# Routed expert tiles of 160 rows instead of 128, with the weights stationary in gate and up

## The chip, the cores and the metric

The kernel runs on one core of a Trainium2 chip. The metric is the device time of one execution in microseconds (us). The engines are TensorE (PE for its matmuls, PEld for its weight loads), VectorE (DVE), ScalarE (ACT), GpSimd (POOL) and SyncE (SP, which here only issues DMAs).

## What is computed

One block of a network on 512 tokens of width 1024: cross-attention, a gated feed-forward with ternary weights, and a mixture of experts. The last part is the one that matters here:

```python
h = _rmsnorm(x, rms_weight)
ht = h.reshape(-1, d)                      # 512 x 1024
topv, topi = jax.lax.top_k(softmax(ht @ router_w), 2)
# w_dense: the two normalised weights of each token, else 0
g = jnp.einsum('td,edf->tef', ht, w_gate)  # 8 experts, 1024 -> 512
u = jnp.einsum('td,edf->tef', ht, w_up)
eo = jnp.einsum('tef,efd->ted', jax.nn.silu(g) * u, w_down)  # 512 -> 1024
moe = jnp.einsum('te,ted->td', w_dense, eo)
sh = jax.nn.silu(ht @ sw_gate) * (ht @ sw_up) @ sw_down      # shared expert
return x + (moe + sh)
```

Each token goes through two of the eight experts, so there are 1024 routed rows. Evaluating the reference's inputs gives 123, 138, 144, 135, 89, 129, 152 and 114 rows for the eight experts.

## The kernel before

**Arithmetic.** Every fp32 operand is split into a high part and a low part (the difference), both stored as fp32r. A product is three matmuls: high x high, high x low, low x high. ScalarE makes the high part of a weight (line L1465, `WH`, by `split`), VectorE the low part (line L980, `WL`).

**Tiles.** The expert stage works in tiles of 128 rows. Tiles 0 to 2 are the shared expert on the first 384 tokens. The routed tiles follow, grouped by expert: an expert with n rows has ceil(n/128) tiles, here 13 in all. The last tile, `total`, is the shared expert on tokens 384 to 511. The numbers of tiles are found on the chip (`CNT`) and steer loops on every engine: an outer loop over the eight experts, an inner loop over the tiles of one. Rows are scattered by token into a DRAM buffer `rows_dram` (GpSimd, line L647) at places that are padded to whole tiles, and the padding is zeroed before by 34 DMAs of 256 KB (line L573). At the end GpSimd gathers two result rows for each token (line L657, `GA` and `GB`) and VectorE adds them, weighted (lines L1172, L1175).

**One routed tile on TensorE** (function `tile` of the tensor block). The rows stand transposed in `ETH` and `ETL` (high, low; 128 x 8 x 128) as the stationary operand, and the weights stream past 512 columns at a time. Gate goes to bank 0 and up to bank 1, each with 16 matmuls of `ETH` (lines L299, L300, by `highs`) and 8 of `ETL` (L305, by `lows`). Then come 4 transposes of the next tile's rows `XG` (L1843), 4 of the hidden values `HE` (L1885), 4 more of `XG`, and the down product: 16 matmuls with `HTH`, 8 with `HTL`, into banks 2 and 3.

**The others in one routed tile.** ScalarE: copies half of the last result to `YS` (L1517), SiLU of gate (L1521), `HTH` (L1526), `ETH` (L1500). VectorE: the other half of `YS` (L1023), gate times up (L994), `HTL` (L1002), `ETL` (L987). After the last tile of an expert both split the next expert's weights, six pieces of 128 x 2048: two for gate, two for up, two for down. ScalarE waits with the two for down until the down product that reads the old ones is done. SyncE stores `YS` and loads `XG` for the tile after next, and loads the weights of the expert after next, one piece as each raw buffer becomes free.

**Order at the seam** between the shared tiles and the first routed one: VectorE subtracts the first half of expert 1's gate weights, does the last shared tile's hidden values, then the second half of the gate weights, then `ETL` of the first routed tile. TensorE waits for each half of the gate weights by itself (`free_c[0]`, `free_c[1]`), and for `ETL` only ahead of the 8 low matmuls.

## Time and profile before

| | |
|---|---|
| median of three runs | 668.27 us (668.19 to 670.72) |
| profiled execution, own time | 670.5 us |
| its span, first to last instruction | 668.7 us |
| mean granted TensorE clock | 0.99 of full |

The routed tiles take 394 to 633 us of the span. Busy shares are means over stages; for one change the waits and the starts of single instructions in its own stage say more. A matmul's recorded duration includes its way through the array, so the distance between the starts of two neighbours is what one costs in a stream.

### The profile page before, as it was taken

Reading aid. Unit: us, or ns where it says so; the run is one execution under the profiler, and the core shown is the slowest. Engines: PE = TensorE matmul, PEld = TensorE weight load, DVE = VectorE, ACT = ScalarE, POOL = GpSimd, SP = SyncE. Lnnn points to the kernel's source line nnn. Section 1 sums busy time; section 2 is a strip of 40 time slices with the busy share of each in tenths; the row PEclk is TensorE's granted clock in tenths of the full one; section 3 lists DMA queues with packets and bytes.
Section 4 is the critical chain, followed back from the end, with each engine's and each line's share of the span. In section 5 each row is a group of like instructions: output and inputs, shape, how many; then the busy total and the mean of one; then the engine's idle time right before and its main releaser. Section 6 shows DMA issues by size and latency. Waiting matters only on the chain.

```text
span 668.7 us, 9683 instructions
## 1 busy us (share of the span) xinstructions
PE 635.5 (95%) x3288; PEld 477.4 (71%) x3289; DVE 488.0 (73%) x789; ACT 413.8 (62%) x538; POOL 144.7 (22%) x140
## 2 busy tenths in 40 slices
PE   6889999998999999969999999999999999999996
PEld 5778888886886444434477877878878788787774
DVE  5788888879687779988898386547291992745886
ACT  3898888789647879875573366254361781816640
POOL 3354445406000334529200400000000000000051
PEclk9899999999999999979999999999999999999999
DMA  8967776765176988529975749929283796482946
GB/s 336 363 276 296 296 289 238 310 269 168 53 261 268 419 346 361 195 86 397 397 301 204 287 181 385 372 79 392 93 333 137 276 390 274 168 334 97 373 162 248
DMA packets 31113, 179.02 MB, mean 268 GB/s; under 512 B 3824, under 2 KB 3824, under 8 KB 14832
## 3 DMA queue, kind: packets, MB, share of 16 engines
q1 hardware_dynamic: 26064, 161.39, 62.4%
q0 software_dynamic: 5024, 17.30, 6.8%
q8 instruction: 14, 0.23, 0.1%
q14 instruction: 11, 0.09, 0.0%
HBM read 155.62 MB, written 23.07 MB: 267 GB/s over the span
## 4 chain that ended last, share of the span: by engine, by line
PE 54%; DVE 17%; ACT 15%; DMA 6%; issue 6%; POOL 1%; SPq 1%; DVEq 1%; POOLq 0%; ACTq 0%
PE BK L299 11%; PE BK L300 11%; PE BK L305 11%; PE BK L293 9%; ACT PR L1280 5%; ACT RA L1253 3%; PE BK L1762 3%; PE BK L1661 2%; DVE WL L980 2%; DMA RA<-wbit 2%; PE BK L1885 2%; DMA GA<-rows,SLOT 2%; DMA RX<-wqk 1%; DVE BH L862 1%; PE BK L1646 1%
## 5 line engine op out<-in xcount | busy, mean ns | idle before, releaser
L299 PE MATMUL BK<-WH,ETH 128*128 128x512 f32 x272 | 107.4, 395 | 1.3 <-ACT ETH L1500 1.3
L300 PE MATMUL BK<-WL,ETH 128*128 128x512 f32 x272 | 106.1, 390 | 0.0
L980 DVE TENSOR_TENSOR WL<-RA,WH 128x2048 fp32r<-128x2048 f32 x40 | 89.4, 2287 | 9.7 <-ACT WH L1465 9.5
L1465 ACT ACTIVATE WH<-RA 128x2048 fp32r<-128x2048 f32 x40 | 73.8, 1923 | 2.3 <-PE BK L1762 2.3
L305 PE MATMUL BK<-WH,ETL 128*128 128x512 f32 x272 | 67.5, 390 | 0.0
L1526 ACT ACTIVATE HTH<-BK 128x256 fp32r<-128x256 f32 x30 | 10.7, 383 | 88.7 <-PE BK L1885 88.6
L299 PEld LDWEIGHTS BK<-WH,ETH 128*128 128x128 f32 x272 | 51.0, 188 | 15.8 <-DVE WL L980 3.3
L657 POOL DMA_INDIRECT GA<-rows,SLOT x4 | 4.9, 1228 | 264.7 <-DVE WL L980 263.8
L305 PEld LDWEIGHTS BK<-WH,ETL 128*128 128x128 f32 x272 | 51.0, 188 | 10.7
L300 PEld LDWEIGHTS BK<-WL,ETH 128*128 128x128 f32 x272 | 51.1, 188 | 10.3
L994 DVE TENSOR_TENSOR HE<-BK,SI 128x256 f32<-128x256 f32 x34 | 12.9, 420 | 57.0 <-PE BK L305 48.3
L625 POOL TENSOR_TENSOR HB<-HB,ND (+2 forms) x28 | 31.1, 1127 | 104.9 <-DVE BH L862 104.2
L1350 ACT ACTIVATE RA<-RA,RT 128x2048 int16<-128x2048 f32 x22 | 44.2, 2018 | 9.6 <-DMA RA<-wbit 6.6
L299 PE MATMUL BK<-WH,HTH 128*128 128x512 f32 x120 | 48.1, 401 | 0.0
L300 PE MATMUL BK<-WL,HTH 128*128 128x512 f32 x120 | 46.9, 391 | 0.0
L980 DVE TENSOR_TENSOR WL<-RC,WH 128x2048 fp32r<-128x2048 f32 x20 | 44.9, 2285 | 0.6 <-ACT WH L1465 0.6
L1716 PE MATMUL BK<-TG,XQ 128*128 128x512 bf16 x192 | 42.4, 379 | 0.1
L1762 PE MATMUL BK<-TD,HQT 128*128 128x512 bf16 x176 | 39.4, 384 | 0.0
L1465 ACT ACTIVATE WH<-RC 128x2048 fp32r<-128x2048 f32 x20 | 37.3, 1920 | 0.6 <-PE BK L305 0.6
L1280 ACT ACTIVATE PR<-BK,RT 128x512 f32<-128x512 f32 (+1 forms) x64 | 32.7, 536 | 6.6 <-DVE RT L729 6.6
L1253 ACT ACTIVATE RA<-RA 128x2048 f32<-128x2048 f32 x19 | 36.2, 1912 | 0.0
L1716 PE MATMUL BK<-TX,XQ 128*128 128x512 bf16 x160 | 35.2, 379 | 0.0
(272 smaller groups left out, 1400.9 us busy)
## 6 DMA issues: line engine op xcount, KB each, us to landing
RA<-wbit SPq DMA_DIRECT2D x54, 1024.0 KB, 6.3
RA<-wmoe SPq DMA_DIRECT2D x40, 1024.0 KB, 6.8
RC<-wmoe SPq DMA_DIRECT2D x20, 1024.0 KB, 7.6
rows<-ZERO POOLq DMA_DIRECT2D x34, 256.0 KB, 12.1
XG<-rows SPq DMA_DIRECT2D x15, 512.0 KB, 7.1
rows<-YS SPq DMA_DIRECT2D x14, 512.0 KB, 6.6
RA<-wqk SPq DMA_DIRECT2D x7, 640.0 KB, 8.1
RA<-wo SPq DMA_DIRECT2D x4, 1024.0 KB, 7.5
```

Source lines behind the costliest of these rows:

```text
L293: m = e.matmul(dst, st, mv, start=first and i == 0 and j == 0, stop=last and i == n - 1 and j == 2)
L299: e.matmul(dst, sh, mh, start=first and i == 0, stop=False)
L300: e.matmul(dst, sh, ml, start=False, stop=False)
L305: m = e.matmul(dst, sl, mh, start=False, stop=i == len(pairs) - 1)
L625: e.tensor_tensor(HB[:, t, cs], HB[:, t, cs], ND[:, cs], ALU.mult).then_inc(s("hnd"), 1)
L980: e.tensor_tensor(WL[m][:, q * RAW:q * RAW + RAW], RC[j][:, :], WH[m][:, q * RAW:q * RAW + RAW].bitcast(f32), ALU.subtract)\
L1253: e.activation(RA[j][:, :], RA[j][:, :], ACT.Abs, accum_out=ACCW[:, column]).then_inc(free_a[j], 1)
L1280: ins = e.activation(PR[h][:, off:off + P * (i + 1)], STR[h][:, off:off + P * (i + 1)], ACT.Exp, bias=NM[:, h, i:i + 1], accum_out=RS[:, h ...
L1350: e.activation(RB16[j], RB[j][:, :], ACT.Copy, scale=SW[:, 0:1]).then_inc(s("rnd"), 1)
L1465: e.activation(WH[m][:, q * RAW:q * RAW + RAW], RC[2 * m + q][:, :], ACT.Copy)\
L1716: m = e.matmul(bank[out], XQ[:, k, t * P:t * P + P], weights[:, k, :], start=k == 0, stop=k == KD - 1)
L1762: m = e.matmul(bank[2 * (t % 2) + q], HQT[t % 2][:, k, :], (TD1[:, k, :] if k < 16 else TD2[:, k - 16, :])[:, q * 512:q * 512 + 512], star ...
```

## The change

A routed tile now has R = 160 rows. An expert has 1 tile for up to 160 rows, so the eight experts have 8 tiles.

- **Gate and up** have the weights stationary (128 x 128 blocks) and stream the rows: `EX` holds for each of the 8 blocks of the width 160 high values and then 160 low ones. Each block of `WH` streams all 320 columns, each block of `WL` the 160 high ones. There are 4 blocks of hidden columns (f) by 8 blocks of width (k), for gate and for up. The result stands transposed already (hidden column by row), so the transposes of `HE` fall away.
- The two halves of each result (high rows and low rows) are added on the way: ScalarE copies one half of gate to `SR`, VectorE adds the other (`gate_sum`), ScalarE takes the SiLU, and VectorE does the product with both halves of up (`routed_product`).
- **Up goes into the banks of gate**, so it waits for `gate_sum` (semaphore `hsum`).
- **Down** has the first 128 rows as before. The last 32 rows' high parts and low parts stand side by side in `HX` and go through as one stationary block of 64 columns against `WH`, plus one of 32 columns against `WL`; both halves are added by `result` on their way out, in `XY`.
- The rows' transposes are 16 in place of 8 (128 rows and 32 rows apart), their loads and the result's stores are two DMAs in place of one.
- A routed tile waits for all of `EX` and for both halves of the gate weights before it starts. At the seam VectorE does `routed_lo(NS)` ahead of the second half of the gate weights, and TensorE does all 16 row transposes ahead of the `HE` transposes. `XG` and `XY` now lie where `H3` lay.
- Zeroing takes 40 DMAs in place of 34.
- The last shared tile waits for both parts of its rows before its first matmul.

```diff
-MAXT = NS + (2 * TOK // P + NE - 1)
+R = 160
+TAIL_R = R - P
+MAXT = NS + NE + (2 * TOK - 1) // R
...
+NZERO = (XT_TILES - NS) * R // (P // 2)
+TK = ((0, 1, 2), (3, 4, 5), (6, 7))
+TB = (0, 1, 3)
+TB_FIRST = (4, 5, 3)
+GBK = (0, 1, 3, 4)
+AB = (2, 5)
...
-        XG = c("XG", [P, DM], f32)
-        assert c.at == TG[0].manual_sbuf_range[0]
+        EX = c("EX", [P, KD, 2, R], f32r)
+        UT = c("UT", [P, 3, R], f32)
+        HX = nc.alloc_sbuf_tensor_at("HX", [P, KE, 2 * R], f32r, offset=HTH.manual_sbuf_range[0])
...
+        SR = Region(a.at)("SR", [P, KE, R], f32)
...
+        XG = kept("XG", [P, DM], f32)
+        XY = kept("XY", [P, DM], f32)
+        XTAIL, YTAIL = slice(0, TAIL_R), slice(TAIL_R, 2 * TAIL_R)
...
+            e.dma_start(rows_dram[bass.ds(row, P), :], H3[:, NS, :]).then_inc(s("x_in3"), 16)
             e.wait_ge(s("rows"), 1)
...
+            e.wait_ge(s("et_pe"), 2 * NS)
+            e.dma_start(XG[:, :], rows_dram[R:R + P, :]).then_inc(s("e_in"), 16)
+            e.wait_ge(s("x_in3"), 32)
+            e.dma_start(XY[XTAIL, :], rows_dram[R + P:2 * R, :]).then_inc(s("e_in"), 16)
...
+            def store(t):
+                row, tail = e.snap((t - NS) * R), e.snap((t - NS) * R + P)
+                waits(e, ("ys_a", t + 1), ("ys_d", t + 1), ("y_st", t * 32 + 32))
+                e.dma_start(rows_dram[bass.ds(row, P), :], YS[:, :]).then_inc(s("y_st"), 16)
+                e.dma_start(rows_dram[bass.ds(tail, TAIL_R), :], XY[YTAIL, :]).then_inc(s("y_st"), 16)
...
-            for half in range(2 * (XT_TILES - NS)):
+            for half in range(NZERO):
...
+            def routed_lo(t, at=TB):
+                for n, ks in enumerate(TK):
+                    e.wait_ge(s("et_hi"), t * 3 + n + 1)
+                    ins = e.tensor_tensor(EX[:, ks[0]:ks[-1] + 1, 1, :], r3(bank[at[n]][:, 0:R * len(ks)], len(ks)),
+                                          EX[:, ks[0]:ks[-1] + 1, 0, :].bitcast(f32), ALU.subtract)
+                    if n != 1:
+                        ins.then_inc(s("et_lo"), 1)
+
+            def gate_sum(t, q):
+                waits(e, ("gate_a", t * 3 + q + 1))
+                v = SR[:, 2 * q:2 * q + 2, :]
+                e.tensor_tensor(v, routed_columns(2 * q, 2, 0), v, ALU.add).then_inc(s("hsum"), 1)
+
+            def routed_product(t):
+                waits(e, ("gate_a", t * 3 + 3))
+                for n, (f, m) in enumerate(((0, 2), (2, 1), (3, 1))):
+                    waits(e, ("up_pe", t * 4 + f + m))
+                    v, u = SR[:, f:f + m, :], UT[:, f % 3:f % 3 + m, :]
+                    e.tensor_tensor(u, routed_columns(f, m, 0), v, ALU.mult)
+                    e.tensor_tensor(v, routed_columns(f, m, 1), v, ALU.mult).then_inc(s("hsum"), 1)
+                    waits(e, ("hsum", t * 5 + n + 3))
+                    ins = e.tensor_tensor(v, u, v, ALU.add)
+                    if n != 1:
+                        ins.then_inc(s("eh"), 1)
+
+            def routed_hidden_lo(t):
+                for q in range(2):
+                    ks = slice(2 * q, 2 * q + 2)
+                    e.wait_ge(s("ht_hi"), t * 2 + q + 1)
+                    ins = e.tensor_tensor(HX[:, ks, R + TAIL_R:2 * R], SR[:, ks, 0:P], HX[:, ks, 0:P].bitcast(f32),
+                                          ALU.subtract)
+                    if q == 0:
+                        ins.then_inc(s("ht_lo"), 1)
+                e.tensor_tensor(HX[:, :, R:R + TAIL_R], SR[:, :, P:R], HX[:, :, P:R].bitcast(f32), ALU.subtract)\
+                    .then_inc(s("ht_lo"), 1)
 
             def hidden_product(t):
-                waits(e, ("esilu", t + 1), ("up_pe", t + 1))
+                waits(e, ("gate_a", t * 3 + 3), ("up_pe", t * 4 + 4))
                 for q in range(2):
                     cs = slice(q * 256, q * 256 + 256)
                     e.tensor_tensor(HE[:, cs], bank[1][:, cs], SI[:, cs], ALU.mult).then_inc(s("eh"), 1)
...
-                e.tensor_copy(YS[:, 512:1024], bank[3]).then_inc(s("ys_d"), 1)
+                waits(e, ("y2_pe", t + 1), ("y_st", t * 32 + 32))
+                e.tensor_copy(YS[:, 512:1024], bank[AB[1]])
+                waits(e, ("ys_a", t + 1))
+                for q in range(2):
+                    v = XY[YTAIL, q * 512:q * 512 + 512]
+                    ins = e.tensor_tensor(v, bank[6 + q][YTAIL, :], v, ALU.add)
+                ins.then_inc(s("ys_d"), 1)
 
             def router_evac(t):
...
             e.wait_ge(s("rows"), 1)
             hidden(NS - 1, HTKH, HTKL)
+            routed_lo(NS, TB_FIRST)
             split(1, 0, (1,))
-            rows_lo(NS)
             split(1, 1)
+            e.sem_inc(s("hsum"), 5 * NS)
 
             def tile(t):
+                gate_sum(t, 0)
                 result(t)
-                hidden(t)
-                rows_lo(t + 1)
+                gate_sum(t, 1)
+                routed_product(t)
+                routed_hidden_lo(t)
...
+            def routed_hi(t, at=TB):
+                for n, ks in enumerate(TK):
+                    if n < 2:
+                        e.wait_ge(s("et_pe"), t * 2 + n + 1)
+                    e.activation(EX[:, ks[0]:ks[-1] + 1, 0, :], r3(bank[at[n]][:, 0:R * len(ks)], len(ks)), ACT.Copy)\
+                        .then_inc(s("et_hi"), 1)
             e.wait_ge(s("d_pe"), 2 * NT)
             split(0, None, (1,), (0,))
...
@@ -1513,30 +1589,48 @@
             split(0, None, (2,), (1,))
 
             def result(t):
-                waits(e, ("y2_pe", t + 1), ("y_st", t * 16 + 16))
-                e.activation(YS[:, 0:512], bank[2], ACT.Copy).then_inc(s("ys_a"), 1)
-
...
-                e.wait_ge(s("gate_pe"), t + 1)
-                e.activation(SI[:, :], bank[0], ACT.Silu).then_inc(s("esilu"), 1)
-                if hi is HTKH:
+                waits(e, ("y2_pe", t + 1), ("y_st", t * 32 + 32), ("et_lo", t * 2 + 2))
+                e.activation(YS[:, 0:512], bank[AB[0]], ACT.Copy)
+                for q in range(2):
+                    ins = e.activation(XY[YTAIL, q * 512:q * 512 + 512], bank[6 + q][XTAIL, :], ACT.Copy)
+                ins.then_inc(s("ys_a"), 1)
+
+            def hidden(t, n, hi=HTH):
+                e.wait_ge(s("gate_pe"), t * 2 + 2)
+                e.activation(SI[:, :], bank[0], ACT.Silu).then_inc(s("gate_a"), 3)
+                if n == NS - 1:
                     split(1, NS, (0,))
...
-                if more:
+                if n < NS - 1:
                     rows_hi(t + 1)
+
             def tile(t):
                 result(t)
-                hidden(t)
-            hidden(0)
+                for q in range(2):
+                    waits(e, ("gate_pe", t * 2 + q + 1))
+                    e.activation(SR[:, 2 * q:2 * q + 2, :], routed_columns(2 * q, 2, 1), ACT.Copy)\
+                        .then_inc(s("gate_a"), 1)
+                for q in range(2):
+                    ks = slice(2 * q, 2 * q + 2)
+                    waits(e, ("hsum", t * 5 + q + 1))
+                    ins = e.activation(SR[:, ks, :], SR[:, ks, :], ACT.Silu)
+                ins.then_inc(s("gate_a"), 1)
+                for q in range(2):
+                    ks = slice(2 * q, 2 * q + 2)
...
-                                    IDF[:, :])
+                    m = e.transpose(bank[4 + q][:, k * P:k * P + P], rows[:, cs], IDF[:, :])
                 m.then_inc(s("et_pe"), 1)
+
+            def routed_rows(t, ns, at=TB):
+                for n in ns:
+                    if n == 0:
+                        waits(e, ("e_in", t * 32 + 32))
+                    for i, k in enumerate(TK[n]):
+                        cs = slice(k * P, k * P + P)
+                        e.transpose(bank[at[n]][:, i * R:i * R + P], XG[:, cs], IDF[:, :])
+                        m = e.transpose(bank[at[n]][:, i * R + P:i * R + R], XY[XTAIL, cs], IDF[XTAIL, XTAIL])
+                    if n != 1:
...
+            def routed_tile(t, gi):
+
+                waits(e, ("et_lo", t * 2 + 2))
+                for m in range(2):
+                    waits(e, (free_c[2 * m], gi + 1), (free_c[2 * m + 1], gi + 1))
+                    for f in range(KE):
+                        if m and f % 2 == 0:
+                            waits(e, ("hsum", t * 5 + f // 2 + 1))
+                        for k in range(KD):
+                            at = slice(k * FE + f * P, k * FE + f * P + P)
+                            if k == KD - 1:
+                                e.matmul(bank[GBK[f]][:, 0:R], WL[m][:, at], EX[:, k, 0, :], start=False, stop=False)
+                            mm = e.matmul(bank[GBK[f]][:, 0:2 * R], WH[m][:, at],
+                                          EX[:, k, :, :].rearrange("p a b -> p (a b)"), start=k == 0, stop=k == KD - 1)
+                            if k < KD - 1:
+                                e.matmul(bank[GBK[f]][:, 0:R], WL[m][:, at], EX[:, k, 0, :], start=False, stop=False)
+                        if m:
+                            mm.then_inc(s("up_pe"), 1)
+                        elif f % 2:
+                            mm.then_inc(s("gate_pe"), 1)
+                waits(e, ("hsum", t * 5 + 3))
+                routed_rows(t + 1, (0, 1))
+                waits(e, ("hsum", t * 5 + 4))
+                routed_rows(t + 1, (2,))
                 waits(e, ("ys_a", t + 1), ("ys_d", t + 1), (free_c[4], gi + 1), (free_c[5], gi + 1))
                 for h in range(2):
                     waits(e, ("ht_hi", t * 2 + h + 1))
                     for q in range(2):
-                        highs(e, bank[2 + q], y_high(h, q), h == 0)
+                        highs(e, bank[AB[q]], [(HX[:, k, 0:P], WH[2][:, down_at(k, q)], WL[2][:, down_at(k, q)])
+                                               for k in (2 * h, 2 * h + 1)], h == 0)
                 e.wait_ge(s("ht_lo"), t * 2 + 2)
                 for q in range(2):
-                    m = lows(e, bank[2 + q], y_low(q))
-                m.then_inc(s("y2_pe"), 1)
+                    lows(e, bank[AB[q]], [(HX[:, k, R + TAIL_R:2 * R], WH[2][:, down_at(k, q)]) for k in range(KE)])
+                for q in range(2):
+                    for k in range(KE):
+                        if k:
+                            e.matmul(bank[6 + q][XTAIL, :], HX[:, k, P:R], WL[2][:, down_at(k, q)], start=False, stop=False)
+                        mm = e.matmul(bank[6 + q][0:2 * TAIL_R, :], HX[:, k, P:R + TAIL_R], WH[2][:, down_at(k, q)],
+                                      start=k == 0, stop=k == KE - 1)
+                        if k == 0:
+                            e.matmul(bank[6 + q][XTAIL, :], HX[:, k, P:R], WL[2][:, down_at(k, q)], start=False, stop=False)
+                mm.then_inc(s("y2_pe"), 1)
...
-            tile(total, NE + 1, None, False)
+            tile(total, NS, NE + 1)
 
 
```

**TensorE, one routed tile: gate.** Before, the start of a tile in the loop (BK is a PSUM bank, WH_145 and WL_146 the gate weights):

```order
L299 MATMUL BK<-WH_145,ETH 128x512
L300 MATMUL BK<-WL_146,ETH 128x512
L299 MATMUL BK<-WH_145,ETH 128x512
L300 MATMUL BK<-WL_146,ETH 128x512
L305 MATMUL BK<-WH_145,ETL 128x512 x8
```

After, the start of a tile, the first of the four blocks f and the change to the second:

```order
L2015 MATMUL BK<-EX,WH_145 128x320
L2018 MATMUL BK<-EX,WL_146 128x160
L2015 MATMUL BK<-EX,WH_145 128x320
L2018 MATMUL BK<-EX,WL_146 128x160
L2014 MATMUL BK<-EX,WL_146 128x160
L2015 MATMUL BK<-EX,WH_145 128x320 x2
```

The 512 columns of weights that streamed past the rows have become 320 and 160 columns of rows that stream past blocks of weights; each matmul loads another block.

**TensorE, the end of a routed tile's down product after** (before, it ended with the row of x8):

```order
L317 MATMUL BK<-WH_141,HX 128x512 x8
L2040 MATMUL BK<-WH_141,HX 64x512
L2043 MATMUL BK<-WL_151,HX 32x512
L2039 MATMUL BK<-WL_151,HX 32x512
L2040 MATMUL BK<-WH_141,HX 64x512
```

The matmuls with 64 and 32 output rows are new, 8 of each in a tile.

**VectorE at the seam** (HE: hidden values of the last shared tile; WL_146: gate weights of the first expert, WL_150 its up weights). Before:

```order
L980 TENSOR_TENSOR WL_146<-RA_95,WH_145 128x2048
L994 TENSOR_TENSOR HE<-BK,SI 128x256 x2
L1002 TENSOR_TENSOR HTKL<-BK,HTKH 128x256 x2
L980 TENSOR_TENSOR WL_146<-RA_96,WH_145 128x2048
L987 TENSOR_TENSOR ETL<-BK,ETH 128x512 x2
L980 TENSOR_TENSOR WL_150<-RA_97,WH_140 128x2048
```

After:

```order
L1004 TENSOR_TENSOR WL_146<-RA_95,WH_145 128x2048
L1054 TENSOR_TENSOR HE<-BK,SI 128x256 x2
L1062 TENSOR_TENSOR HTKL<-BK,HTKH 128x256 x2
L1017 TENSOR_TENSOR EX<-BK,EX 128x3x160 x2
L1017 TENSOR_TENSOR EX<-BK,EX 128x2x160
L1004 TENSOR_TENSOR WL_146<-RA_96,WH_145 128x2048
L1004 TENSOR_TENSOR WL_150<-RA_97,WH_140 128x2048
```

The second half of the gate weights has moved behind the low part of the first routed tile's rows.

## Rows read from the trace of the kernel before

**Rows 1.** The page's part 1: busy time, share of the span, instructions.

```profile
PE 635.5 (95%) x3288; PEld 477.4 (71%) x3289; DVE 488.0 (73%) x789; ACT 413.8 (62%) x538; POOL 144.7 (22%) x140
```

**Rows 2.** Busy time by stretch: engines, clock, DMA share, GB/s; inside the routed tiles.

```profile
420.00:440.00 20.00, 19.85 (x94) 16.29 (x93) 7.37 (x10) 2.90 (x6) 0.00 (x0) 1.00 0.73 297
```

**Rows 3.** Groups by line and shape, 405.2 to 625.7 us (twelve routed tiles).

```profile
L1843 PE MATMUL BK<-IDF,XG 128*128 128x128 f32 x96 | 14.4, 272 | 0.0
...
L980 DVE TENSOR_TENSOR WL<-RA,WH 128x2048 fp32r<-128x2048 f32 x28 | 62.3, 2287 | 7.0 <-ACT WH L1465 7.0
L1465 ACT ACTIVATE WH<-RA 128x2048 fp32r<-128x2048 f32 x28 | 51.4, 1927 | 0.0
...
L987 DVE TENSOR_TENSOR ETL<-BK,ETH 128x512 fp32r<-128x512 f32 x24 | 15.5, 686 | 0.8
...
L1500 ACT ACTIVATE ETH<-BK 128x512 fp32r<-128x512 f32 x24 | 13.0, 600 | 0.0
...
L994 DVE TENSOR_TENSOR HE<-BK,SI 128x256 f32<-128x256 f32 x24 | 9.1, 420 | 47.8 <-PE BK L305 47.0
```

**Rows 4.** Timeline (start, us): first and last routed tile's end of up; what follows.

```profile
405.21 0.60 PE L1843 MATMUL BK<-IDF,XG 128*128 128x128 f32 x4
...
625.78 0.60 PE L1843 MATMUL BK<-IDF,XG 128*128 128x128 f32 x4
...
628.57 5.54 ACT L1465 ACTIVATE WH<-RA 128x2048 fp32r<-128x2048 f32 x3
630.53 4.49 DVE L980 TENSOR_TENSOR WL<-RA,WH 128x2048 fp32r<-128x2048 f32 x2 [1.00 <-ACT WH L1465]
...
631.25 1.98 PE L305 MATMUL BK<-WH,HTL 128*128 128x512 f32 x8
...
633.07 0.40 PE L299 MATMUL BK<-WH,ETH 128*128 128x512 f32 x1
```

**Rows 5.** Timeline of PE in narrow windows: attention matmuls of falling width (L1661).

```profile
64.89 0.46 PE L1661 MATMUL BK<-PTH,VH 128*128 128x384 f32 x2
...
65.06 0.46 PE L1661 MATMUL BK<-PTH,VH 128*128 128x256 f32 x3
...
65.18 0.46 PE L1661 MATMUL BK<-PTH,VH 128*128 128x256 f32 x3
...
65.47 0.44 PE L1661 MATMUL BK<-PTH,VL 128*128 128x512 f32 x1
...
65.75 0.57 PE L1661 MATMUL BK<-PTH,VL 128*128 128x512 f32 x2
```

**Rows 6.** Timeline at the seam: last shared tile into first routed tile.

```profile
390.95 0.60 PE L1843 MATMUL BK<-IDF,XG 128*128 128x128 f32 x4
...
391.24 0.76 DVE L994 TENSOR_TENSOR HE<-BK,SI 128x256 f32<-128x256 f32 x2 [0.76 <-PE BK L305]
...
393.29 2.29 DVE L980 TENSOR_TENSOR WL<-RA,WH 128x2048 fp32r<-128x2048 f32 x1
...
394.20 0.49 PE L299 MATMUL BK<-WH,ETH 128*128 128x512 f32 x1 [1.27 <-ACT ETH L1500]
```

**Rows 7.** PE's longest idle time (timeline), and busy time with clock just then.

```profile
289.54 2.72 PE L1756 MATMUL BK<-IDB,HQ 128*128 128x128 bf16 x19 [5.41 <-DVE HQ L966]
...
290.00:294.00 4.00, 3.83 (x25) 2.32 (x23) 2.85 (x5) 3.29 (x4) 0.00 (x0) 0.52 0.55 233
```

**Rows 8.** Timeline of the end: last subtractions ahead of the gathers, first gather, last wait.

```profile
635.94 4.49 DVE L980 TENSOR_TENSOR WL<-RA,WH 128x2048 fp32r<-128x2048 f32 x2
...
641.39 2.10 POOL L657 DMA_INDIRECT GA<-rows,SLOT  x1 [263.81 <-DVE WL L980]
...
661.83 1.28 DVE L1172 SCALAR_TENSOR_TENSOR XRES<-GA,RT,XRES 128x1024 f32<-128x1024 f32 x1 [1.18 <-DMA GA<-rows,SLOT]
```

**Rows 9.** Zeroing: its DMAs (page, part 6), and busy time just behind them.

```profile
rows<-ZERO POOLq DMA_DIRECT2D x34, 256.0 KB, 12.1
...
334.00:337.00 3.00, 3.00 (x22) 2.10 (x20) 3.00 (x3) 1.18 (x1) 0.00 (x0) 1.00 0.15 31
```

More of the change, by code:

```diff
@@ L1557, in _ @@
             split(NE + 1, total, (2,))
-            hidden(total, False)
+            hidden(total, NS)
         @blk.tensor
@@ L1856, in routing, with tile @@
                     logits_t()
-            def tile(t, gi, rows=None, more=True):
-                waits(e, ("et_hi", t * 2 + 2), (free_c[0], gi + 1))
+            def tile(t, n, gi):
+                more = n < NS
+                waits(e, ("et_hi", t * 3 + 3), (free_c[0], gi + 1))
+                if not more:
+                    waits(e, ("et_lo", t * 2 + 2))
                 for m in range(2):
@@ L1863, in tile @@
                             waits(e, (free_c[2 * m + q], gi + 1))
[L1864 removed]
+                        highs(e, bank[m], [(EX[:, k, 0, 0:P], WH[m][:, k * FE:k * FE + FE], WL[m][:, k * FE:k * FE + FE])
                                            for k in range(4 * q, 4 * q + 4)], q == 0)
[L1866 removed]
+                        if n == 0:
                             routing((m, q))
                     e.wait_ge(s("et_lo"), t * 2 + 2)
[L1869 to L1871 removed]
+                    lows(e, bank[m], [(EX[:, k, 1, 0:P], WH[m][:, k * FE:k * FE + FE]) for k in range(KD)])\
+                        .then_inc(s(("gate_pe", "up_pe")[m]), (2, 4)[m])
+                    if n == 0:
                         routing((m, 2))
[L1873 to L1874 removed]
+                if n < NS - 1:
+                    rows_t(0, H3[:, n + 1, :])
+                elif more:
+                    e.wait_ge(s("ys_d"), NS)
+                    routed_rows(NS, (0, 1, 2), TB_FIRST)
                 else:
@@ L1877, in tile @@
                     kept_result(HT1H, HT1L, 2)
-                if isinstance(t, int) and t == 0:
+                if n == 0:
                     ranks()
@@ L1945, in _ @@
             for t in range(NS):
[L1946 removed]
+                tile(t, t, 0)
             e.wait_ge(s("cnt"), 1)
```

118 lines of the change are left out of this document (55 added, 63 removed).

## The prediction

> **What bounds the kernel now.** I read the page first: TensorE is busy 95% of the span [rows 1]. Then busy time by stretch inside the routed tiles: 19.85 of 20 us, clock 1.00, DMA share 0.73 [rows 2]. So in the stage that changes TensorE is the bound, and the others matter only where they make it wait. The groups by line there show how VectorE waits for TensorE: 47.8 us ahead of gate times up [rows 3]. The timeline gives the price: the end of up comes at 405.21 us in the first routed tile and at 625.78 in the thirteenth, so one tile takes 220.57 / 12 = 18.38 us; the first routed gate matmul starts at 394.20 [rows 6] and the last down product ends at 633.07 [rows 4]. Thirteen tiles take 238.9 us.
>
> **The change, first the number of tiles.** Of the expected row counts (123, 138, 144, 135, 89, 129, 152, 114) five lie above 128 and none above 160: 13 tiles become 8.
>
> **Prices of a matmul.** I take the distance of starts. Eight of 512 columns take 633.07 - 631.25 = 1.82, so 0.23 each [rows 4]. 384 columns cost 0.17 and 256 cost 0.12; from 65.18 to 65.75 lie one of 256, two of 128 and one of 512, which leaves 0.22 for the two narrow ones: 0.11 each [rows 5]. The row transposes, also 128 wide, cost (0.60 - 0.27) / 3 = 0.11 as well [rows 3, 4]. The slope between 256 and 512 columns is 0.43 ns a column, so 128 columns alone would need 0.06: below some 250 columns the loading of the next weight block sets the pace, at 0.11. For the new shapes: 320 columns lie between 256 and 384, 0.145; 160 columns get the floor, 0.11. Both matmuls of a pair load a new block, so a pair costs 0.255. Bounds: 0.215 if the narrow one cost only its columns (0.07), 0.29 if the two cost as 384 and 256 (0.17, 0.12).
>
> The Trainium skill, "TensorE: Matmul & The Clock Gate", section "Back-to-back issue gap", has about 81 ns for a load and a matmul of 128 columns in a stream, and 131 ns for 512. The trace says 110 and 230, so the measurement decides.
>
> **TensorE in a new tile.** Gate 32 pairs 8.15, up 8.15; row transposes 16 x 0.11 = 1.75; down as before 24 x 0.23 = 5.5; the new tail of down 16 x 0.23 = 3.7 (512 columns stream past 64 or 32 columns of weights, which costs as much as past 128). Sum 27.25. The HE transposes and the wait ahead of them are gone.
>
> **The others in a new tile.** Let T be the moment at which up is issued. VectorE costs 0.42 for 256 and 0.69 for 512 columns, so 0.49 for 320, 0.32 for 160, 0.65 for 480; ScalarE 0.60 for 512 and 1.93 for 2048, so 0.44 for 320 and 0.57 for 480 [rows 3]; weight pieces in a row take 2.2 on VectorE (4.49 for two) and 1.8 on ScalarE (5.54 for three) [rows 4].
> - T + 0.3 the last up matmul is out (0.40 recorded) [rows 4]. VectorE: two products and an add for the last 160, until T + 1.35. ScalarE: high part of the hidden values T + 1.8, then three pieces of EX, T + 3.45.
> - TensorE transposes until T + 1.75 and needs the hidden values then: no wait of note. Down lasts until T + 10.95.
> - VectorE: low parts until T + 4.4, then waits for ScalarE's first weight piece (3.45 + 1.9 = T + 5.4). Both gate pieces are through at T + 9.9, 1 us ahead of the next gate at T + 10.95. This is what hides them; without it each us late costs 1 us in each of 8 tiles.
> - ScalarE's pieces for down wait for T + 11.2 and take until T + 15.
> - VectorE's six pieces end at T + 18.7, and only then comes `gate_sum`, T + 19.2. TensorE ends gate at T + 19.1 and must wait for it, since up goes into the same banks: a wait of 0.1 to 0.2. The second `gate_sum`, behind three operations of 0.69, ends near T + 21.8; up's third block needs it at T + 23.4.
> So a tile takes 27.5, with VectorE just behind TensorE. Eight take 220.0: **-18.9**.
>
> Loads and stores: a weight piece is asked for at T + 7.7 at the earliest and T + 18.7 at the latest, and used 27.5 us after its predecessor; the extra DMAs for the tails stand in SP's queue behind waits that are over early. The DMA share was 0.73 with a faster cycle [rows 2]. Nothing.
>
> **The seam.** Before, the last shared tile's up ends at 390.95, VectorE subtracts the second half of the gate weights from 393.29 to 395.6, and gate has started at 394.20, since it needed that half later and ETL later still [rows 6]. After: 16 transposes until 392.7, seen at 393.0; ScalarE's remaining EX pieces (0.57, 0.44) until 394.0, its hidden halves until 394.7; VectorE's HTKL until 395.2, EX low 1.7, until 396.9, second half of the gate weights 2.3, until 399.2. Gate starts at 399.3: **+5.1** (bounds 4 and 6).
>
> That leaves TensorE idle for about 6 us (393.3 to 399.3). Its one comparable idle time was 5.41 us, and in the work behind it the granted clock was 0.52, the 1.2 GHz level, over the stretch 290 to 294 [rows 7]. Four us at half pace give back two: **+2.0** (bounds 0 and 4).
>
> **The end.** Before, the last two pieces ahead of the gathers run from 635.94 to 640.43, and the first gather starts at 641.39 [rows 8]; against the end of down (633.07) that is 7.4 and 8.3 later. After, VectorE's result waits for three ScalarE copies (0.3 + 3 x 0.6, less overlap: 1.8), then two adds (1.3), then two pieces (4.5): 7.8. The end waits for the gathers (661.83) [rows 8], so **+0.5**. The last shared tile's own wait for its rows' low parts (T + 4.4 against T + 10.95) is covered by the long down product.
>
> **Zeroing.** Six more DMAs of 256 KB are 1.6 MB behind 8.9; behind them the DMA share falls to 0.15 for 3 us [rows 9], which takes them up. Nothing (bound 1).
>
> **The sum.** +5.1 + 2.0 - 18.9 + 0.5 = -11.3. Against its own execution (span 668.7, time 670.5) this is a span of 657.4 and a time of 659.2. That execution was 2.2 above the median 668.27, so I forecast 657.0.
>
> **The rivals.**
> - **A: as summed**, 657. Its own range 652 to 664: the seam and the clock 3 either way, 0.3 a tile for the small operations.
> - **B: the narrow matmul hides its weight load under the wide one before it.** For it: two loads of 0.11 just fit into 0.215. Against it: in rows 5 a 128-wide matmul behind others costs 0.11. Gate then ends at T + 17.8, `gate_sum` still at T + 19.2, up takes 6.9: a cycle of 26.1, 11 less in all: 646. By the skill's 81 ns the pair would be about 0.22 and the result much the same.
> - **C: VectorE becomes the bound (slower).** Place: the first `gate_sum` behind six subtractions. Between T and T + 19.2 stand 13 further short operations on two engines that hand over to each other; a hand-over that costs 0.1 to 0.2 more than I allow comes straight on TensorE's wait, in 8 tiles. From 1.4 us a tile the gain is gone. At 2 us: 673. For it: no slack. Against it: the hand-over HE to TensorE is short now and VectorE's durations are steady.
> - **D: pairs at their upper price**, 0.29: 2.2 a tile, 17.9 in all: 675. Rows 5 speak against it.
> - **E: small sums**: a longer time at the low clock, DMAs that land late, a stall at each loop border: 665 to 669.
>
> **How the numbers follow.** A 0.62, B 0.12, C 0.12, D 0.06, E 0.08. The likeliest is A. The range 646 to 669 takes in A, B and E and leaves out C and D, near 2 in 10. Half a per cent, 3.3 us, is about what a measurement of this kernel can tell from no change; within it lie 665 to 671.6. That has E and the upper edge of A: 0.13. Slower: C and D, 0.17. Faster: 0.70.
>
> **What would show it.** Right: 8 ends of up 27.5 apart; starts of 320 and 160 wide matmuls 0.145 and 0.11 apart; first routed gate matmul near 399.3 behind an idle time of 6 us, at a clock near 0.5; TensorE's only repeated wait a small one for `gate_sum`. Wrong: pairs of 0.215 or 0.29; TensorE waits of over 1 us a tile for `gate_sum`, for the gate weights or for EX; a clock that falls again inside the tiles; waits for DMA.

## The result, and the profile after

The changed kernel takes 683.66 us (median of 4 runs, 683.05 to 685.42) against 668.96 (4 runs) of the kernel before: ratio 1.022, 95% interval 1.0191 to 1.025. It is slower: the interval lies above 1. The forecast was 657.0, range 646 to 669: the time lies outside the range, on the other side of no change.

The profiled execution has a span of 683.6, 14.9 longer than before. First the page's part 1; it answers to [rows 1].

```profile
PE 649.1 (95%) x3663; PEld 498.8 (73%) x3677; DVE 513.6 (75%) x861; ACT 424.6 (62%) x559; POOL 148.3 (22%) x146
```

TensorE is the bound as before. Of its longest waits in the changed kernel (us in total, times, longest) only the middle row belongs to the routed tiles, and that one stands at the seam. Inside the routed tiles it waits for nobody: from 420 to 640 us it is busy 20.00 of every 20 us.

```profile
PE BK L1664 <- ACT WVH L1274: 6.5, 1, 6.5
PE BK L2015 <- DVE WL L1004: 5.3, 1, 5.3
PE BK L1850 <- DVE HQ L990: 5.2, 1, 5.2
```

So the time is in TensorE's own work. The timeline of TensorE after (start, duration) shows one whole tile: gate starts, the row transposes start, down starts, its last 32 rows start, the next gate starts. The last row is the end of the eighth tile.

```profile
433.93 0.31 PE L2015 MATMUL BK<-EX,WH 128*128 128x320 f32 x1
434.08 0.24 PE L2018 MATMUL BK<-EX,WL 128*128 128x160 f32 x1
434.15 0.35 PE L2015 MATMUL BK<-EX,WH 128*128 128x320 f32 x1
434.34 0.24 PE L2018 MATMUL BK<-EX,WL 128*128 128x160 f32 x1
...
450.41 0.27 PE L1944 MATMUL BK<-IDF,XG 128*128 128x128 f32 x1
450.61 0.24 PE L1945 MATMUL BK<-IDF,XY 32*128 32x32 f32 x1
450.79 0.33 PE L1944 MATMUL BK<-IDF,XG 128*128 128x128 f32 x1
451.05 0.24 PE L1945 MATMUL BK<-IDF,XY 32*128 32x32 f32 x1
451.22 0.33 PE L1944 MATMUL BK<-IDF,XG 128*128 128x128 f32 x1
...
453.82 0.50 PE L311 MATMUL BK<-WH,HX 128*128 128x512 f32 x1
...
456.10 0.63 PE L311 MATMUL BK<-WH,HX 128*128 128x512 f32 x1
456.53 0.63 PE L312 MATMUL BK<-WL,HX 128*128 128x512 f32 x1
...
458.02 0.39 PE L312 MATMUL BK<-WL,HX 128*128 128x512 f32 x1
458.25 0.39 PE L311 MATMUL BK<-WH,HX 128*128 128x512 f32 x1
...
460.97 0.39 PE L2040 MATMUL BK<-WH,HX 128*64 128x512 f32 x1
...
464.65 0.31 PE L2015 MATMUL BK<-EX,WH 128*128 128x320 f32 x1
...
648.97 0.39 PE L311 MATMUL BK<-WH,EX 128*128 128x512 f32 x1
```

Reading the differences of starts, beside what was forecast:

| part of a tile | measured | forecast |
|---|---|---|
| gate and up, 128 matmuls | 450.41 - 433.93 = 16.48 | 16.3 |
| 16 row transposes | 453.82 - 450.41 = 3.41 | 1.75 |
| down, 24 matmuls | 460.97 - 453.82 = 7.15 | 5.5 |
| down, last 32 rows, 16 matmuls | 464.65 - 460.97 = 3.68 | 3.7 |
| tile | 30.72 | 27.5 |

Two parts are wrong, and by the same size. A 32-row transpose starts 0.26 behind the 128-row one ahead of it (450.79 to 451.05), and the next 128-row one 0.17 behind that (451.05 to 451.22): 0.43 for a pair that was forecast at 0.22. And matmuls of 512 columns in the down product lie 0.43 apart (456.10 to 456.53), where 0.23 was forecast and is measured a moment later (458.02 to 458.25). Busy time by stretch after shows the clock in both. The columns are the stretch, its length, PE, PEld, DVE, ACT, POOL, the granted clock, the DMA share and GB/s; the stretches are gate and up, the transposes, the first part of down, and the rest of down.

```profile
444.00:450.40 6.40, 6.40 (x52) 6.40 (x51) 2.26 (x6) 0.47 (x1) 0.00 (x0) 1.00 0.66 252
450.40:453.80 3.40, 3.40 (x17) 2.06 (x16) 2.41 (x7) 0.93 (x2) 0.00 (x0) 1.00 0.00 0
454.40:457.80 3.40, 3.40 (x10) 2.65 (x8) 2.20 (x3) 3.40 (x4) 0.00 (x0) 0.50 0.63 193
458.00:464.60 6.60, 6.60 (x30) 4.37 (x29) 6.60 (x4) 4.03 (x3) 0.00 (x0) 1.00 0.65 245
```

Behind the transposes the clock is at the 1.2 GHz level for 3.4 us, in every one of the eight tiles (it falls at 423.6, 454.4, 485.1, 515.8, 546.5, 577.3, 608.0 and 638.7), although PE counts as busy all through. Look also at PEld in the second row: 2.06 of 3.40, where gate and up have 6.40 of 6.40. During the mixed transposes the weight loads no longer lie end to end. In the busy times that is the only sign of the loss.

The pair of gate and up costs what was forecast, 16.48 / 64 = 0.2575 against 0.255, but not in the way that was forecast. From the start of a 320-wide matmul to the next start lie 0.19 (434.15 to 434.34) in place of 0.145, and from a 160-wide one 0.07 (434.08 to 434.15) in place of 0.11. Both loads of a pair lie end to end there (PEld 6.40 of 6.40). The sum came out right and the split did not; what sets the split was not looked at.

At the seam, which answers to [rows 6], the timeline after reads:

```profile
390.70 0.27 PE L1944 MATMUL BK<-IDF,XG 128*128 128x128 f32 x1
...
394.11 0.65 PE L1993 MATMUL BK<-IDF,HE 128*128 128x128 f32 x4
...
395.43 0.76 DVE L1062 TENSOR_TENSOR HTKL<-BK,HTKH 128x256 fp32r<-128x256 f32 x2 [3.67 <-ACT HTKH L1606]
...
396.10 1.61 DVE L1017 TENSOR_TENSOR EX<-BK,EX 128x480 fp32r<-128x480 f32 x3
...
397.62 4.49 DVE L1004 TENSOR_TENSOR WL<-RA,WH 128x2048 fp32r<-128x2048 f32 x2
...
400.05 0.60 PE L2015 MATMUL BK<-EX,WH 128*128 128x320 f32 x1 [5.29 <-DVE WL L1004]
```

Gate starts at 400.05, 5.85 later than before, behind an idle time of 5.29; the order of VectorE's steps is the forecast's, each 0.7 to 1.0 late, because the 16 transposes end at 394.11 in place of 392.7. The clock is low until 406.6, and the first tile's gate and up take 19.58, 3.1 more than the others'.

The budget of the span against the forecast of 657.4: transposes 8 x 1.66 = 13.3; low clock in down 8 x 1.65 = 13.2; gate and up 8 x 0.18 = 1.4; clock behind the seam 1.1; seam 0.75; no wait for `gate_sum` -2.0 (8 x 0.25); the end -1.5. Sum 26.2, and 657.4 + 26.2 = 683.6.

### The profile page after: what moved, and what is told of

Read it like the earlier page. It is cut to its first block, busy times and chain, and to the rows that moved or that the text cites. A ratio compares the mean times of both kernels' runs of the same rounds, so it can differ in the third digit from the quotient of the medians.

```text
span 683.6 us, 10567 instructions
## 1 busy us (share of the span) xinstructions
PE 649.1 (95%) x3663; PEld 498.8 (73%) x3677; DVE 513.6 (75%) x861; ACT 424.6 (62%) x559; POOL 148.3 (22%) x146
## 4 chain that ended last, share of the span: by engine, by line
PE 61%; DVE 15%; ACT 12%; DMA 4%; issue 4%; POOL 1%; SPq 1%; DVEq 0%; POOLq 0%; ACTq 0%
PE BK L2015 14%; PE BK L305 9%; PE BK L2018 5%; PE BK L311 5%; ACT PR L1349 5%; PE BK L312 4%; PE BK L317 3%; PE BK L1755 3%; PE BK L1856 3%; PE BK L1944 3%; PE BK L2040 2%; PE BK L1945 2%; DVE WL L1004 2%; PE BK L2039 2%; DMA RA<-wbit 2%
## 5 line engine op out<-in xcount | busy, mean ns | idle before, releaser
L2015 PE MATMUL BK<-EX,WH 128*128 128x320 f32 x512 | 134.7, 347 | 5.3 <-DVE WL L1004 5.3
L2018 PE MATMUL BK<-EX,WL 128*128 128x160 f32 x448 | 106.9, 239 | 0.0
L2015 PEld LDWEIGHTS BK<-EX,WH 128*128 128x128 f32 x512 | 93.9, 192 | 6.2 <-issue 5.5
L2018 PEld LDWEIGHTS BK<-EX,WL 128*128 128x128 f32 x448 | 87.2, 195 | 0.3
L1625 ACT ACTIVATE HX<-SR 128x320 fp32r<-128x320 f32 x16 | 7.5, 471 | 57.6 <-DVE SR L1035 57.6
L1032 DVE TENSOR_TENSOR UT<-BK,SR 128x160 f32<-128x160 f32 (+1 forms) x24 | 9.1, 380 | 39.1 <-PE BK L2015 39.1
L1810 PEld LDWEIGHTS BK<-TG,XQ 128*128 128x128 bf16 x192 | 18.6, 98 | 22.5 <-ACT XQ L1412 0.6
L311 PE MATMUL BK<-WH,HX 128*128 128x512 f32 x64 | 33.4, 523 | 0.0
L607 POOL TENSOR_TENSOR WQH<-RA,ONEF 128x768 fp32r<-128x768 f32 (+1 forms) x14 | 22.1, 1576 | 51.2 <-DMA RA<-wqk 43.4
L1856 PEld LDWEIGHTS BK<-TD,HQT 128*128 128x128 bf16 x176 | 17.4, 100 | 20.8 <-issue 1.7
```

Source lines behind the costliest of these rows:

```text
L311: e.matmul(dst, sh, mh, start=first and i == 0, stop=False)
L1810: m = e.matmul(bank[out], XQ[:, k, t * P:t * P + P], weights[:, k, :], start=k == 0, stop=k == KD - 1)
L1856: m = e.matmul(bank[2 * (t % 2) + q], HQT[t % 2][:, k, :], (TD1[:, k, :] if k < 16 else TD2[:, k - 16, :])[:, q * 512:q * 512 + 512], star ...
L2015: mm = e.matmul(bank[GBK[f]][:, 0:2 * R], WH[m][:, at], EX[:, k, :, :].rearrange("p a b -> p (a b)"), start=k == 0, stop=k == KD - 1)
L2018: e.matmul(bank[GBK[f]][:, 0:R], WL[m][:, at], EX[:, k, 0, :], start=False, stop=False)
```

## The experiments

**e1_full_rows: transposes of one shape.** The 32 tail rows are loaded into the last 32 partitions of `XY`, and the transpose reads all 128 partitions of it; the 96 columns that nobody wants are overwritten by the transpose of `XG` that follows. The number of matmuls, of weight loads and of bytes moved by DMA stays.

```diff
-                e.dma_start(XY[XTAIL, :], rows_dram[bass.ds(tail, TAIL_R), :]).then_inc(s("e_in"), 16)
+                e.dma_start(XY[XIN, :], rows_dram[bass.ds(tail, TAIL_R), :]).then_inc(s("e_in"), 16)
...
-                        e.transpose(bank[at[n]][:, i * R:i * R + P], XG[:, cs], IDF[:, :])
-                        m = e.transpose(bank[at[n]][:, i * R + P:i * R + R], XY[XTAIL, cs], IDF[XTAIL, XTAIL])
+                        e.transpose(bank[at[n]][:, i * R + TAIL_R:i * R + R], XY[:, cs], IDF[:, :])
+                        m = e.transpose(bank[at[n]][:, i * R:i * R + P], XG[:, cs], IDF[:, :])
```

> The changed kernel (683.7), but the transposes of the last 32 rows read all 128 partitions of their tile (the 32 rows moved to its upper end, the rest is overwritten), so that all 16 row transposes have one shape. Theory 1, the change between 128-row and 32-row weight loads is what makes 16 transposes take 3.41 us, and this slow stretch is what the clock falls after: transposes 1.75 us, no fall of the clock in the down products, a tile of 27.4 us, eight times 3.3 less: about 657. Theory 2, the clock falls because of the load-bound gate and up matmuls or of the half-empty tail of down: transposes 1.75 us, but the down product still has its 3.4 us at the low level, a tile of 29.1: about 670.

Measured: 656.98 us (654.8 to 657.76), ratio to before 0.9807 (0.9784 to 0.9831); span 655.3. The 16 transposes take 1.67, the clock stays at 1.00 inside the tiles, down takes 5.57, a tile 27.40 (428.31 to 455.70). Busy time by stretch of this kernel, transposes and the down product behind them:

```profile
444.80:446.40 1.60, 1.60 (x16) 1.60 (x16) 1.22 (x4) 0.46 (x2) 0.00 (x0) 1.00 0.00 0
446.50:450.00 3.50, 3.50 (x18) 2.87 (x17) 2.61 (x6) 3.50 (x5) 0.00 (x0) 1.00 0.53 184
```

PEld is busy 1.60 of 1.60. One edit takes away both losses, 3.3 us a tile and 26.7 us in all: without the mixed transposes the clock does not fall inside the tiles either.

**e2_grouped: the same transposes, sorted by shape.** In each of the three groups first those of 128 rows, then those of 32: 5 changes of shape inside the stretch in place of 15.

```diff
                         e.transpose(bank[at[n]][:, i * R:i * R + P], XG[:, cs], IDF[:, :])
+                    for i, k in enumerate(TK[n]):
+                        cs = slice(k * P, k * P + P)
                         m = e.transpose(bank[at[n]][:, i * R + P:i * R + R], XY[XTAIL, cs], IDF[XTAIL, XTAIL])
```

> The changed kernel, but in each group of blocks the 128-row transposes come first and then the 32-row ones: 6 changes of shape in place of 16. Theory 1a, each change between the shapes costs about 0.2 us: the 16 transposes take about 2.4 us. Theory 1b, a 32-row transpose is slow by itself whatever stands next to it: 3.4 us as before. The clock falls less or not at all if the length of the stretch decides: 662 to 676; at 1b 683.

Measured: 659.14 (one run), below the 662 that was expected at least; transposes 2.10 a tile (2.4 expected), no fall of the clock inside the tiles. TensorE's timeline of this kernel:

```profile
499.97 0.49 PE L1944 MATMUL BK<-IDF,XG 128*128 128x128 f32 x3
500.39 0.37 PE L1947 MATMUL BK<-IDF,XY 32*128 32x32 f32 x3
500.69 0.55 PE L1944 MATMUL BK<-IDF,XG 128*128 128x128 f32 x3
501.17 0.37 PE L1947 MATMUL BK<-IDF,XY 32*128 32x32 f32 x3
501.47 0.44 PE L1944 MATMUL BK<-IDF,XG 128*128 128x128 f32 x2
501.83 0.31 PE L1947 MATMUL BK<-IDF,XY 32*128 32x32 f32 x2
```

From the first of 128 rows to the first of 32 it takes 0.42; two steps of 0.11 in it leave 0.20 for the change. (In the second group 501.17 - 500.69 = 0.48 leave 0.26.) Three of 32 rows and the change back take 500.69 - 500.39 = 0.30; with 0.17 for the change back, as in the changed kernel, those among their own kind cost some 0.07. It is the change between the two kinds of transpose that costs, not the small transpose.

**e3_filler: the mixed stretch cut by dense matmuls.** Four matmuls of 512 columns, into banks that are overwritten later, stand behind the first and behind the second group of mixed transposes of each tile.

```diff
+            def filler():
+                for q in range(2):
+                    for u in range(2):
+                        e.matmul(bank[6 + q], WH[1][:, 0:P], WH[1][:, 0:512], start=True, stop=True)
...
-                routed_rows(t + 1, (0, 1))
+                routed_rows(t + 1, (0,))
+                filler()
+                routed_rows(t + 1, (1,))
+                filler()
```

> The changed kernel with 8 more dense matmuls of 512 columns in each routed tile (1.84 us of work whose result is overwritten), four behind the first and four behind the second group of row transposes. Theory 1, the unbroken slow stretch makes the clock fall: it falls no more or less, and a tile gets 0.2 us longer at most: 680 to 686, though work was added. Theory 2, gate and up or the tail are the cause: the clock falls as before and each tile is 1.84 longer: about 698.

Measured: 686.55 (one run; 680 to 686 expected), mean clock 0.990 against 0.967. The stretch with its fillers takes 1.24 + 1.03 + 1.24 + 1.03 + 0.81, down 5.57, a tile 31.08. Busy time by stretch of this kernel, over the transposes and over down:

```profile
450.40:456.00 5.60, 5.60 (x26) 3.94 (x26) 2.18 (x6) 2.22 (x5) 0.00 (x0) 1.00 0.07 11
456.20:460.00 3.80, 3.80 (x18) 3.14 (x17) 2.73 (x3) 3.80 (x3) 0.00 (x0) 1.00 0.40 148
```

The clock no longer falls inside the tiles, so 2.06 us of useless work a tile cost only 0.36 (the run is still 2.9 us slower than the changed kernel). The mixed transposes themselves still cost their 0.43 a pair.

**e4_before_short: the mixing put into the kernel before.** Six transposes of 32 rows are added between those of 128 in each routed tile; they write what the next one overwrites.

```diff
+                    if rows is None and k < 3:
+                        e.transpose(bank[4 + q][:, k * P + P:k * P + P + 32], XG[0:32, cs], IDF[0:32, 0:32])
```

> The kernel before (668.3) with six 32-row transposes added per routed tile between the 128-row ones of the rows (results overwritten): nothing of the change but this mix. Theory 1: each costs about 0.3 us beyond nothing, 1.9 to 2.6 a tile, and the clock falls behind them for up to 1.7 more: 13 tiles, 693 to 722, mean clock under 0.98. Theory 2: 693 to 702 and no fall of the clock inside the routed tiles.

Measured: 686.88 (one run), below both expected ranges. The twelve transposes of a tile (8 of rows, 4 of `HE`) and the wait among them take 3.17 with the six added ones, in place of 1.76: 0.235 net for each. TensorE's timeline, of the kernel before and then of this one:

```profile
441.92 0.60 PE L1843 MATMUL BK<-IDF,XG 128*128 128x128 f32 x4
442.67 0.77 PE L1885 MATMUL BK<-IDF,HE 128*128 128x128 f32 x4
```

```profile
445.43 0.27 PE L1843 MATMUL BK<-IDF,XG 128*128 128x128 f32 x1
445.63 0.24 PE L1846 MATMUL BK<-IDF,XG 32*128 32x32 f32 x1
...
446.84 0.60 PE L1887 MATMUL BK<-IDF,HE 128*128 128x128 f32 x4
```

Before, four row transposes (0.44) and a wait of 0.31 lie ahead of `HE`. With three small ones among them the four take 446.84 - 445.43 = 1.41, so each added one costs (1.41 - 0.44) / 3 = 0.32, as in the changed kernel (0.43 - 0.11), and covers part of that wait. So the price is there without anything else of the change. The clock did not fall in any tile: the mixing by itself is not enough for that.

**e5_double: as long a stretch, but of one shape.** In e1's kernel each of the 16 transposes is issued twice, to the same place.

```diff
+                        for u in range(2):
```

> The kernel with full row transposes (e1_full_rows), in which each of the 16 transposes of a routed tile is issued twice, to the same place: 32 transposes of one shape at 0.105 each, a stretch of about 3.4 us, as long as the mixed one in the changed kernel (3.41), but without gaps. The output is not changed. Question: is it the length of the stretch of transposes that makes the granted clock fall in the down product, or the gaps at the changes of shape? Theory 'stretch' (transposes as such, however dense, bring the fall once the stretch is 3.4 long): the clock falls early in each down product as in the changed kernel, 1.65 a tile; tile 27.4 + 1.7 + 1.65 = 30.75, total near 657.0 + 8 x 3.35 = 684. Theory 'gaps': no fall inside the tiles, tile 29.1, total 657.0 + 13.6 = 670.5. I lean to 'gaps' at 0.55, since e4_before_short had a stretch of 3.17 without a fall, but that is close in length too.

Measured: 672.6 us (671.85 to 672.68), ratio 1.0044 (1.0026 to 1.0062). The 32 transposes take 3.41, to the hundredth as long as the 16 mixed ones. Busy time by stretch of this kernel:

```profile
448.00:451.40 3.40, 3.40 (x33) 3.40 (x33) 2.41 (x7) 0.93 (x2) 0.00 (x0) 1.00 0.00 0
451.50:455.00 3.50, 3.50 (x18) 2.87 (x17) 1.62 (x3) 3.30 (x4) 0.00 (x0) 1.00 0.60 172
```

The clock stays at 1.00 and down takes 5.57; a tile takes 29.14. So neither the length of the stretch nor transposes as such bring the fall here; the mixing does. The Trainium skill, "TensorE: Matmul & The Clock Gate", section "Part 4: PE-mode transpose", says that transposes do not count as activity of TensorE in the way that matmuls do; by that alone the clock should fall here as well. It did not in any of the eight tiles.

**e6_best and e7_seam_alone: VectorE's order at the seam.** The second half of the gate weights goes ahead of the last shared tile's low parts, in e1's kernel and in the changed one.

```diff
-            hidden(NS - 1, HTKH, HTKL)
-            routed_lo(NS, TB_FIRST)
+            hidden_product(NS - 1)
             split(1, 0, (1,))
+            hidden_lo(NS - 1, HTKH, HTKL)
+            routed_lo(NS, TB_FIRST)
```

> Full row transposes (as e1_full_rows) and one change of order on VectorE at the seam: the second half of the first routed tile's gate weights is subtracted between the last shared tile's hidden product and its low parts, and the low part of the first routed tile's rows comes last. In e1_full_rows the first routed gate matmul starts at 398.79 behind an idle time of 5.4, which ends with that second half of the gate weights. Theory 'seam' (VectorE's order decides that start): the first gate starts about 2.2 earlier, near 396.6, the idle time is about 3 and the rest of the tiles as in e1_full_rows; time 657.0 - 2.2 = 654.8, and about 1 less if the shorter idle time also shortens the stretch at the low clock (396.4 to 403.2 before): 653.8. Rival: the last shared tile's down product, which now waits for its low parts behind the subtraction of 2.3, hands the whole gain back: 657.

> The same order on VectorE at the seam as in e6_best, put into the changed kernel with its mixed transposes. Theory: gate starts near 397.8 in place of 400.05; the 3.41 of transposes and the 1.65 of low clock in each tile stay; 683.7 - 2.2 = 681.5. Rival: the clock's fall inside the tiles depends on what happened at the seam (it would go with a shorter idle time there): then 681.5 - 13.2 = 668.

Measured: e6_best 655.27 us (654.28 to 655.79), ratio 0.9786 (0.977 to 0.9803), the fastest of all here. TensorE's idle time at the seam is 3.3 in place of 5.4, 2.1 less, where 2.2 was expected; this execution comes to the seam 0.6 later, so the first gate starts at 397.32 (e1: 398.79). The clock stays low until 403.65 (e1: 403.23), so 6.3 us of the first tile lie at the low clock in place of 4.4, which gives 0.9 back: the second tile starts at 427.70 against 428.31. The span is 654.0 against 655.3; the other 0.7 of it lies behind the last routed tile, where nothing was changed. The gain in time is 1.7 by the medians, less than the 2.2 to 3.2 expected, and since the intervals of e1 and e6 overlap, it is not clear of noise. e7_seam_alone: 682.39 (2 runs), first gate at 398.41, and the clock falls in all eight tiles as before. A shorter idle time at the seam (3.2 in place of 5.3) does not take the falls away.

**e8_before_mixed8 and e9_before_block: can the kernel before be made to lose its clock?** e8 adds 8 transposes of 32 rows, and two of 128, scattered over both groups of a tile; e9 adds 8 pairs in one piece behind the first transpose.

```diff
+                    if rows is None and q == 0 and k == 0:
+                        for n in range(8):
+                            e.transpose(bank[4][:, P:P + 32], XG[0:32, cs], IDF[0:32, 0:32])
+                            e.transpose(bank[4][:, 0:P], XG[:, cs], IDF[:, :])
```

> The kernel before, with more mixing than in e4_before_short: in the row transposes of each routed tile 8 of 32 rows (6 there) and 2 more of 128 rows are added, each of 32 rows between two of 128 rows. The output is not changed. By the price of e4_before_short (0.235 for each of 32 rows) and 0.105 for each of 128 the transposes of a tile take 1.76 + 8 x 0.235 + 2 x 0.105 = 3.85, longer than the 3.41 behind which the clock falls in the changed kernel. Theory 'mixing brings the fall, once there is enough of it': the clock falls in each routed tile behind them, and a tile takes 18.38 + 2.1 + 1.6 = 22.1, the run 670 + 13 x 3.7 = 718. Rival 'it needs something else of the changed kernel' (here transposes of the hidden values stand between the groups, and the down product follows): no fall, tile 20.5, 670 + 13 x 2.1 = 697.

> The kernel before, with one unbroken stretch of mixed transposes: in the first group of row transposes of each routed tile, behind the first of 128 rows, 8 pairs of a 32-row and a 128-row one are added, to the same places. The output is not changed. In e8_before_mixed8 the mixed transposes of a tile took 4.05 but stood in two stretches of some 1.8 with uniform transposes between them, and the clock fell in one tile of thirteen; in the changed kernel one stretch of 3.41 brings the fall in every tile. By 0.43 for a pair the added ones take 3.4 in one piece; tile 18.38 + 3.4 = 21.8. Theory 'unbroken stretch': the clock falls in every routed tile just behind it and costs another 1.6: tile 23.4, run 668 + 13 x 5.0 = 733. Rival 'something else of the changed kernel (its narrow gate and up matmuls ahead of the stretch, say)': no fall or one, tile 21.8, run 668 + 13 x 3.4 = 712.

Measured: e8 701.27 (one run). The transposes of a tile (those of `HE` among them) take 4.05, where 3.85 was expected; the clock falls in one tile of thirteen, the first. e9 717.18 (one run): transposes 4.85, tiles of 21.3 to 21.6 where the clock holds and of 22.7 to 22.8 where it falls, in five of thirteen. Busy time by stretch of e9, behind the block of a tile without a fall and behind that of one with:

```profile
412.50:415.80 3.30, 3.30 (x15) 2.70 (x16) 2.29 (x5) 3.30 (x4) 0.00 (x0) 1.00 0.99 391
454.40:457.70 3.30, 3.30 (x14) 2.91 (x12) 2.14 (x4) 2.84 (x5) 0.00 (x0) 0.50 0.11 35
```

Both theories missed: the fall can be had in the kernel before, with transposes alone, but not in every tile, although each tile issues the same instructions.

## Why the prediction was wrong

- **The step that failed: "row transposes 16 x 0.11".** The 0.11 was read from transposes of 128 rows that stand among themselves [rows 3, 4] and laid on a sequence in which 128 and 32 rows alternate, of which the trace of before had none. Measured: 0.43 a pair, 3.41 a tile. e1, e2 and e4 show that the change between the two kinds of transpose is the price (0.32 for each small one put between large ones in the kernel before). An operation that no row shows wants a bound on both sides; this term was given as known, with none.
- **The second loss hung on the first: the clock.** The forecast counted a low clock once, at the seam, since it took an idle TensorE to be what lowers it [rows 7]. It fell in each tile behind mixed transposes with PE at 100% busy, 1.65 a tile. That in this kernel it takes an unbroken stretch of mixed transposes is shown (e1, e3, e5); why it comes in each tile is not. "A clock that falls again inside the tiles" stood among the signs of being wrong, but in no rival and with no price.
- **No rival had the mechanism.** The slower cases, C and D, were VectorE's `gate_sum` and the pair at 0.29. Neither happened: TensorE waits for no `gate_sum`, here or in e1, where the tile is 27.40, and the pair costs 0.2575, 1% above the forecast of 0.255. The 0.17 left for slower was given for the wrong reasons.
- **Right, by their size:** 8 tiles; tail 3.68 (3.7); the pair, with 0.2575 far from rival B's 0.215 (e1's is the same), though its split into 0.145 and 0.11 was wrong; no wait for loads.
- **Mis-sized, small:** the seam +5.85 (+5.1), again the transposes; with them mended (e1) it is +4.6. The clock behind the seam 3.1 (2.0); in e1 2.1. The end -1.0 (+0.5): the first gather starts 657.80 - 648.97 = 8.8 behind the last down product, as forecast, but from there the span ends after 25.8 in place of 27.3, which the forecast had as unchanged. And the wait for `gate_sum`, 0.25 a tile with rounding, did not come.
- With the two failed terms taken out the sum comes within 2.1 us: e1 has -13.4 of span where -11.3 was forecast. From 668.7: seam +4.6, clock +2.1, tiles 8 x 27.40 - 238.9 = -19.7, end -0.4. That e1's median of 656.98 is the forecast 657.0 to the tenth is luck: the forecast also took off 2.2 us, because the profiled execution of before lay that far above its median, and that of e1 does not.

**Open.** Why the same mixed stretch lowers the clock in every tile of the changed kernel, in five of thirteen in e9, in one in e8 and in none in e4. TensorE's instructions are the same in each tile of e9. The transfers beside them do not decide it. Busy time over the transposes of four tiles of e9, with, without, with and without a fall:

```profile
450.35:455.20 4.85, 4.85 (x26) 3.48 (x25) 0.75 (x2) 0.38 (x1) 0.00 (x0) 0.91 0.00 0
494.43:499.28 4.85, 4.85 (x30) 3.37 (x28) 0.87 (x3) 0.53 (x2) 0.00 (x0) 1.00 0.00 0
515.97:520.82 4.85, 4.85 (x24) 3.46 (x23) 0.91 (x3) 0.00 (x0) 0.00 (x0) 0.83 1.02 412
582.97:587.82 4.85, 4.85 (x29) 3.36 (x28) 0.86 (x3) 0.53 (x2) 0.00 (x0) 1.00 1.01 422
```

The fall comes and stays away at a DMA share of 0.00 and at one of 1.0. The moment at which the stretch comes also differs from tile to tile; no run here changes that alone. And these runs do not separate the number of rows read from other properties of the 32-row transpose, such as its 32 streamed columns. Two things speak for the rows: the 64- and 32-column weight blocks of the tail, at 128 rows, cost no change (0.23 each beside one another), and matmuls of 320 and 160 streamed columns alternate at about the forecast price.

## What to carry to other kernels

- Take the price of an instruction from a row in which it has the same neighbours. A small transpose or matmul between large ones can cost more than a large one: here making the 32-row transposes full (four times the data, three quarters thrown away) turned a loss of 2.2% into a gain of 1.9%. If the shapes must differ, sort them.
- PE "100% busy" does not say that the work is dense. Look at the distance of starts, and, among short matmuls that each load a block, at PEld beside PE: over the same 16 transposes it is 1.60 of 1.60 in e1 and 2.06 of 3.40 here, and the granted clock just behind is worth a look. Among matmuls of 512 columns PEld lies below PE without any loss (2.87 of 3.50 in e1's down product), so there it says nothing.
- Where a kernel loses its clock without idle time, dense work put in between can be nearly free (e3: 2.06 us of it for 0.36). It is no gain by itself; taking the mixing away is.
